# The low half of h made on GpSimd instead of VectorE, in the last stage of a quantise-and-attend convolution pair

## What is computed

```python
# layer 0
im = relu(x) as (C, N*H*W); mn = mean(im, axis=1)
p = clip(u.T @ (im - mn), -clampVal, clampVal)
p = round((p - dmin) * scale) / scale + dmin      # scale = 255 / (dmax - dmin), per channel
y = u @ p; y = y - mean(y, axis=1) + mn
# layer 1, for each sample
h = relu(bn(w_conv1 @ y))                         # 256 channels
d = relu(bn(w_dr @ h + b_dr))                     # 128 channels
cov = (d - mean(d)) @ (d - mean(d)).T / M
att = sigmoid(w_fc @ r(cov) + b_fc)
out = y * att
```

## Time and profile before

| | |
|---|---|
| median of 3 runs | 2085.18 us |
| span of the profiled execution, first to last instruction | 2073.7 us |
| what lies around it, by the median | 11.5 us |
| PE busy | 1748.1 us, 84% |
| DVE busy | 1603.7 us, 77% |
| ACT busy | 1535.3 us, 74% |
| POOL busy | 460.3 us, 22% (all in stage one) |

### The profile page before, as it was taken

How to read it: one execution, slowest core, us unless ns; L and a number is a source line. 1 busy time by engine, 2 the same in 40 slices (tenths; PEclk the granted TensorE clock), 3 DMA queues, 4 the chain that set the end, 5 groups by cost and what they waited for, 6 DMA issues and landing times.

```text
span 2073.7 us, 39111 instructions
## 1 busy us (share of the span) xinstructions
PE 1748.1 (84%) x13384; PEld 1586.6 (77%) x13384; DVE 1603.7 (77%) x2709; ACT 1535.3 (74%) x2025; POOL 460.3 (22%) x135
## 2 busy tenths in 40 slices
PE   8999999999900000089999999999999999999998
PEld 8999999999900000068888888888888888888887
DVE  6888888888878889877777777777777777777774
ACT  7777777777688987557777777777777777777776
POOL 7888888888600000000000000000000000000000
PEclk9999999999955555599999999999999999999999
DMA  9999989989698999702132231313223131231314
GB/s 333 375 328 359 376 310 374 374 315 371 260 360 339 391 384 426 327 25 94 78 148 84 105 128 77 155 77 132 101 81 151 77 153 79 108 124 77 155 64 187
DMA packets 95806, 438.59 MB, mean 211 GB/s; under 512 B 8481, under 2 KB 9633, under 8 KB 80673
## 3 DMA queue, kind: packets, MB, share of 16 engines
q1 hardware_dynamic: 95776, 438.21, 55.2%
HBM read 219.82 MB, written 218.37 MB: 211 GB/s over the span
## 4 chain that ended last, share of the span: by engine, by line
PE 55%; DVE 2%; ACT 0%; DMA 0%; issue 0%
PE y_ps L841 18%; PE z_ps L791 17%; PE d_ps L821 14%; PE cov_ps L805 5%; DVE hl L967 1%; PE ch_ps L849 1%; PE ch_ps L831 0%; DVE g L953 0%; PE ch_ps L832 0%; DVE gg L961 0%; DVE gg L959 0%; PE cov_ps L808 0%; DMA q<-q_scratch 0%; ACT yo L901 0%; DVE qr L920 0%
## 5 line engine op out<-in xcount | busy, mean ns | idle before, releaser
L267 POOL TENSOR_TENSOR xl<-xs,xh 128x1568 fp32r<-128x1568 f32 x128 | 459.4, 3590 | 97.4 <-ACT xh L227 97.4
L901 ACT ACTIVATE yo<-y_ps,attb,att 128x512 f32<-128x512 f32 (+2 forms) x448 | 316.6, 723 | 159.2 <-PE y_ps L841 147.2
L872 ACT ACTIVATE h<-z_ps,sb_h,s_h 128x512 f32<-128x512 f32 (+2 forms) x448 | 317.3, 724 | 85.2 <-PE z_ps L791 72.4
L841 PE MATMUL y_ps<-qr,udh 128*128 128x512 f32 (+2 forms) x896 | 347.8, 390 | 2.0 <-ACT yo L901 1.8
L953 DVE SCALAR_TENSOR_TENSOR g<-d_ps,late 128x512 f32<-128x512 f32 (+1 forms) x224 | 141.8, 633 | 247.4 <-PE d_ps L821 247.4
L791 PE MATMUL z_ps<-qr,wh 128*128 128x512 f32 (+2 forms) x896 | 331.6, 372 | 1.2 <-DVE qr L920 1.2
L791 PE MATMUL z_ps<-qr,wl 128*128 128x512 f32 (+2 forms) x896 | 328.2, 368 | 0.0
L841 PE MATMUL y_ps<-qr,udl 128*128 128x512 f32 (+2 forms) x896 | 327.5, 367 | 0.0
L227 ACT ACTIVATE xh<-xs 128x1568 fp32r<-128x1568 f32 x128 | 194.1, 1517 | 139.9 <-PE pp L284 139.8
L821 PE MATMUL d_ps<-vh,hh 128*128 128x128 f16 (+1 forms) x1600 | 282.2, 220 | 4.0 <-DVE hl L967 4.0
L821 PE MATMUL d_ps<-vh,hl 128*128 128x128 f16 (+1 forms) x1600 | 281.1, 219 | 0.0
(11 more groups left out here) (153 smaller groups left out, 3304.7 us busy)
## 6 DMA issues: line engine op xcount, KB each, us to landing
xs<-in_x_dram SPq DMA_DIRECT2D x128, 784.0 KB, 6.7
out_dram<-yo SPq DMA_DIRECT2D x31, 3136.0 KB, 9.2
pt<-p_scratch SPq DMA_DIRECT2D x56, 1568.0 KB, 9.3
p_scratch<-po_low SPq DMA_DIRECT2D x56, 784.0 KB, 7.6
p_scratch<-late SPq DMA_DIRECT2D x56, 784.0 KB, 7.7
q<-q_scratch SPq DMA_DIRECT2D x32, 784.0 KB, 5.0
q_scratch<-qt SPq DMA_DIRECT2D x28, 784.0 KB, 10.8
q_scratch<-q_res SPq DMA_DIRECT2D x8, 392.0 KB, 8.0
```

The source lines that it names most:

```text
L267: nc.gpsimd.tensor_tensor(xl[:, k % 2], xs[:, k], xh[:, k % 2].bitcast(F32), ALU.subtract).then_inc(split_done, 1)
L841: last = nc.tensor.matmul(y_ps[:, m, 0:widths[c]], part[:, k, m * P:(m + 1) * P], qr[:, slot, k, columns(c)], start=k == 0 and part is udh ...
L872: nc.scalar.activation(h32[:, par, m, 0:w], z_ps[:, m, 0:w], ACT.Relu, scale=s_h[:, m:m + 1], bias=sb_h[:, m:m + 1]).then_inc(z_read, 1)
L901: nc.scalar.activation(yo[:, slot, m, columns(c)], y_ps[:, m, 0:widths[c]], ACT.Identity, scale=att[:, m:m + 1], bias=attb[:, m:m + 1]).th ...
```

## The change

POOL gets a program in the last stage that waits for hh_done, makes hl and adds one to h_split, for each chunk. DVE's program loses the same wait and the same operation. Buffers, the operation's form and everything else stay.

```diff
--- before.py
+++ after.py
@@ -904,6 +904,20 @@
 
                 phases(act, phase)
 
+            @block.gpsimd
+            def _(pool):
+                def phase(r2, a):
+                    for s in range(CH):
+                        g = first_chunk(r2, a) + s
+                        if exists(r2, a):
+                            par, w = (CH * a + s) % 2, widths[s]
+
+                            pool.wait_ge(hh_done, g + 1)
+                            nc.gpsimd.tensor_tensor(hl[:, par, :, 0:w], h32[:, par, :, 0:w], hh[:, par, :, 0:w],
+                                                    ALU.subtract).then_inc(h_split, 1)
+
+                phases(pool, phase)
+
             @block.vector
             def _(dve):
                 steps = [0]
@@ -960,12 +974,6 @@
                             dve.wait_ge(gh_done, g)
                             nc.vector.tensor_tensor(gg[0:dq, 1 - par, 0:dt, P:2 * P], g32[0:dq, 0:dt],
                                                     gg[0:dq, 1 - par, 0:dt, 0:P], ALU.subtract).then_inc(g_split, 1)
-                        if exists(r2, a):
-                            w = widths[s]
-
-                            dve.wait_ge(hh_done, g + 1)
-                            nc.vector.tensor_tensor(hl[:, par, :, 0:w], h32[:, par, :, 0:w], hh[:, par, :, 0:w],
-                                                    ALU.subtract).then_inc(h_split, 1)
                         if s == 2 and exists(r2, a, back=1):
 
                             dve.wait_ge(spread_done, n)
```

## The result

The changed kernel takes 2121.47 us (median of 4, 2118.95 to 2123.41) against 2084.45 (2076.1 to 2085.76) for the kernel before on the same chip: a ratio of 1.0184, with a 95% interval of 1.0158 to 1.0209, 37 us slower. The forecast was 2153 (2088 to 2195), slower.

The account below looks back on a forecast made before the run. PE was taken to bound the last stage; removing DVE's work gains 0, while gg held up by POOL makes PE 2.2 us late in each of 31 samples, 68 us on 2085.2, giving 2153 us (2088 to 2195).

Parts of the forecast that it names:

- What bounds: Last stage: PE busy all 36.56 us a sample; relieving DVE gives back at most 6.8 us, taken as 0.
- The full wait of DVE's cast, gg and weighted sums: Last stage: these and the q conversion wait until POOL's subtraction ends; g and the 384 cast do not.
- The duration of POOL's operation: hl on POOL: 2.35 us for 1024 elements, 1.76 for 768, 1.47 for 640; ends 2.0 to 3.6.
- rival 3: Float16 makes POOL's 1024 form 3.2 us; with exclusion 4.8 us a sample, 2235 us; over 2195, chance 0.1.
- The sum: Last-stage timetable of PE's lateness for gg: 1.8 to 2.5 us a sample, 2.2 taken, times 31 is 68 us.
- the narrow step: Timetable place where z and y are narrow: gg at 19.4, PE wants it at 18.3, 1.1 us late.
- the third: Third lateness, the gg after the weighted sums and q conversion: ends 25.45, wanted at 25.16, 0.3 us late.
- The dead heat at chunk 5: Last lateness: POOL's hl and gg start together; gg 0.7 us late if POOL is first, otherwise 0; half taken.
- What lies around the span: Median of the runs taken as 11.5 us above the profiled execution's span, 2085.2 against 2073.7.
- The signs: Profile after: PE waits 50 to 70 us for gg, longest over 1 us, hardly any for hl; period 38.7 us.
- 1 (no exclusion): POOL reads beside DVE at no cost and hl is in time: 2085 us, or 2078 at best; chance 0.14.
- rival 2: Partial loss: slower POOL without exclusion (2095), or only gg or cast held (2120); 2090 to 2130 us, chance 0.2.

Follow-up runs that it names:

- e9: Kernel before, DVE's hl kept, plus POOL making the same subtraction into a spare tile nobody reads: 2195.3 us against 2082.46, ratio 1.0551.
- e10: Kernel before, DVE's hl kept, plus a POOL memset of 2048 float32 per chunk that nobody reads: 2136.43 us, ratio 1.0269.

## Why the prediction came out as it did

- **What bounds.** Right: PE, with a quarter of DVE's time free and nothing to win from relief (4 us at most were on hl).
- **The full wait of DVE's cast, gg and weighted sums.** Right, and now shown: cast, weighted sums and gg stretched by POOL's run, g and the 384 cast untouched, and e9 has the loss without hl's coming from POOL. The Trainium skill, "SBUF — State Buffer", section "Who interferes with whom", has it as measured here, including that a POOL operation that only writes leaves a two-input operation alone (e10: gg of 384 at 559 ns) and not a two-port one (1079). It says too that who starts first wins: at chunk 5 POOL itself took 2.19 us in place of 1.66.
- **The duration of POOL's operation.** This is the term that was mis-sized: 2.35 us forecast by proportion, 2.15 measured; 1.76 against 1.66 (unheld, e9), 1.47 against 1.41. Between 640 and 1024 elements it grows by (2151 - 1414) / 384 = 1.92 ns an element above 0.19 us fixed, and by that the 1568 elements of the earlier trace rows would take 3.2, not 3.59: the operation with a float16 input and output is cheaper than the float32 one of stage one, where rival 3 feared it dearer. Whether the type or the other stage makes the difference, no run separates.
- **The sum.** With 2.15 the same timetable gives: POOL from 4.54 to 6.69, gg at 7.85, 0.17 late (measured 0.18); at the narrow step POOL until 17.8, gg at 18.95 against 18.08, 0.87 late (measured 0.81); the third, 0.3, shrinks to 0.15 at most (measured 0), since all comes earlier; the last, taken as half of 0.7, is half of 0.54 (measured 0.27). 1.26, less the 0.06 by which hl had been late before, in place of 2.2 a sample; the 0.2 us an operation counts at each meeting, and 0.94 x 31 = 29 us is most of the 31.5 us by which 2153 was too high. The loss of 37 us is little more than half of the 68 forecast.
- **The dead heat at chunk 5.** Its place was right, its victim wrong: not gg but hl is late, because behind gg, which is in first in both samples above, the conversion of q, a double-rate operation too, gets in ahead of POOL in every other sample. That its size came near (0.35 forecast, 0.27 measured) is luck.
- **What lies around the span.** I took 11.5 us, from a median and a span of different executions. Of the changed kernel the profiled execution took 2121.85 us for a span of 2119.9, so about 2 us lie around it, and the span of before was one of the short executions, near the 2076.1 at the low end. It did no harm, since the sum went on top of the median.
- **"DVE busy 243 us less, unless the hold-up is booked as busy time."** It is: 4 us less.
- **The signs.** 50 to 70 us of PE's waits for gg were to be seen, three or four times a sample: it is 24.4 us in 38 waits, 0.18 + 0.81 us a sample by the starts of the products, because the third lateness is not there and the others are shorter. "Hardly any for hl" failed: 7.4 us.
- **Rivals.** 1 (no exclusion) and 3 (a dear operation) are out by the durations above; so is "only gg, or only the cast" under rival 2, since both are held. That 2120 stood there as "half of the sum", so near to the measured time, is chance.

## What to carry to other kernels

Before work is moved from DVE to GpSimd, list which DVE operations would run beside it: those with two SBUF inputs (beside a GpSimd operation that reads SBUF) and those at double rate wait for GpSimd's whole instruction; here the single-rate ones with one SBUF input, alone or beside a PSUM input, didn't. Then price the move by the slack of what follows the held operation, place by place (here three of seven places carried all of the loss, three none), not by busy time, which hides a hold. Shorter GpSimd pieces did no harm here where long ones did: half of hl on each engine (1.17 us on GpSimd in place of 2.15) kept PE fed, and is as fast as the kernel before or 0.1 to 0.3% faster.

## What the runs showed of the hardware that I had not expected

- A held DVE operation's record starts at its turn and is stretched: the 512 cast shows 1.75 us for 0.43, and ends 0.29 us after POOL's operation does. Idle time and waits name nothing.
- A POOL memset, which reads nothing, holds a double-rate cast (1079 against 427 ns) but not a subtraction with two SBUF inputs (gg of 384: 559 ns, 558 before, 983 with the change).
- POOL's float32 minus float16 to float16 subtraction costs 1.92 ns an element and 0.19 us (640 to 1024 elements); by that 1568 elements would take 3.2 us, where the float32 form of stage one takes 3.59.
- A GpSimd operation is also the loser where DVE's two-port operation starts first: 2.19 us in place of 1.66 for 768 elements.
